# A vision-tower kernel on one core: the inverse root of both variances as one GpSimd power

## The reference

```python
h = _L0_tok_ref(x, L0_tok_channel_weights)          # sums of 16x16 patches, then 12 -> 192
h = h + _L0_attn_ref(_layernorm(h, axis=-1), L0_attn_W_qkv, L0_attn_b_qkv)
h = h + _L0_ffn_ref(_layernorm(h, axis=-1), ...)    # 192 -> 768, GELU, 768 -> 192
# _layernorm: (x - m) / sqrt(v + 1e-05)
```

## Time and profile before

| | |
|---|---|
| median of the runs | 500.92 us (500.5 to 501.59) |
| the profiled execution | 501.24 us |
| its span | 499.4 us |
| TensorE matmul busy | 426.2 us, 85% |
| VectorE busy | 415.4 us, 83% |
| ScalarE busy | 311.1 us, 62% |
| GpSimd busy | 338.3 us, 68% |
| moved by DMA | 166.74 MB, mean 334 GB/s |
| granted TensorE clock, mean | 0.952 |

### The profile page before, as it was taken

The page is one execution under the profiler, slowest core; times in us unless marked ns, Lnnn a source line. Parts: engine busy times, 40 slices in busy tenths (PEclk is TensorE's granted clock), DMA queues, the critical chain, the costliest instruction groups (busy, mean ns, idle before and its releaser), DMA issues.

```text
span 499.4 us, 10230 instructions
## 1 busy us (share of the span) xinstructions
PE 426.2 (85%) x3794; PEld 369.5 (74%) x3794; DVE 415.4 (83%) x392; ACT 311.1 (62%) x765; POOL 338.3 (68%) x637
## 2 busy tenths in 40 slices
PE   3994792878989898989898989898989898998897
PEld 2743451567878787879797878787878787887797
DVE  2767779999999999999999999999999999823100
ACT  1012021658686777777777777786868686868572
POOL 2021614286868686868787877878787868687981
PEclk9999556599999999999999999999999999999899
DMA  7999999999999999999999999999999993000011
GB/s 244 349 388 405 407 406 405 405 401 394 391 384 405 404 407 396 405 394 408 401 407 391 406 401 406 396 407 406 406 398 406 399 406 122 29 22 29 21 50 50
DMA packets 54028, 166.74 MB, mean 334 GB/s; under 512 B 6031, under 2 KB 6812, under 8 KB 53978
## 3 DMA queue, kind: packets, MB, share of 16 engines
q1 hardware_dynamic: 53978, 166.08, 85.8%
HBM read 156.42 MB, written 9.63 MB: 333 GB/s over the span
## 4 chain that ended last, share of the span: by engine, by line
DVE 68%; PE 18%; issue 6%; ACT 3%; POOL 3%; DMA 1%; SPq 1%; DVEq 0%; POOLq 0%
DVE pooled L414 52%; PE ps L577 16%; DVE phat_tok L453 5%; DVE stat L444 5%; DVE stat L435 1%; DMA xs<-x 1%; DVE prod L432 1%; DVE stat L446 1%; DVE stat L426 1%; ACT probs_t L960 1%; DVE prod L423 1%; DVE stat L447 1%; POOL stat L1110 0%; POOL newton L1106 0%; POOL newton L1108 0%
## 5 line engine op out<-in xcount | busy, mean ns | idle before, releaser
L414 DVE TENSOR_REDUCE pooled<-xs 128x28 f32<-128x1792 f32 x192 | 329.9, 1776 | 9.2 <-DMA xs<-x 9.2
L1158 POOL TENSOR_TENSOR h_lo<-h_f,h_hi 128x448 fp32r<-128x448 f32 (+1 forms) x192 | 193.1, 1033 | 68.9 <-ACT h_hi L1010 68.8
L577 PE MATMUL ps<-w_hi,h_hi 128*112 128x192 f32 x672 | 183.0, 272 | 0.4 <-POOL h_lo L1158 0.4
L577 PE MATMUL ps<-w_hi,h_lo 128*112 128x192 f32 x672 | 176.0, 262 | 0.0
L577 PE MATMUL ps<-w_lo,h_hi 128*112 128x192 f32 x672 | 176.0, 262 | 0.0
L577 PEld LDWEIGHTS ps<-w_hi,h_hi 128*112 128x112 f32 x672 | 119.8, 178 | 8.7 <-issue 7.2
L1009 ACT ACTIVATE h_f<-ps 128x448 f32<-128x448 f32 (+1 forms) x192 | 98.0, 511 | 37.8 <-PE ps L577 35.7
L577 PEld LDWEIGHTS ps<-w_lo,h_hi 128*112 128x112 f32 x672 | 119.7, 178 | 1.7
L577 PEld LDWEIGHTS ps<-w_hi,h_lo 128*112 128x112 f32 x672 | 120.2, 179 | 0.0
L1010 ACT ACTIVATE h_hi<-ps 128x448 fp32r<-128x448 f32 (+1 forms) x192 | 98.1, 511 | 0.0
L577 PE MATMUL ps<-uhat_stack,f_stack 128*128 128x448 f32 (+1 forms) x192 | 76.6, 400 | 1.4 <-ACT h_hi L1010 1.4
(11 more groups left out here) (144 smaller groups left out, 607.5 us busy)
## 6 DMA issues: line engine op xcount, KB each, us to landing
xs<-x SPq DMA_DIRECT2D x336, 448.0 KB, 7.6
out<-out_sb SPq DMA_DIRECT2D x16, 336.0 KB, 8.5
out<-out_sb SPq DMA_DIRECT2D x16, 252.0 KB, 6.7
out_sb<-wfc SPq DMA_DIRECT2D x1, 576.0 KB
wproj_sb<-wproj SPq DMA_DIRECT2D x1, 576.0 KB
wqkv_sb<-wqkv SPq DMA_DIRECT2D x1, 432.0 KB
cf<-const_full SPq DMA_DIRECT2D x1, 400.5 KB, 3.3
h_f<-const_paired SPq DMA_DIRECT2D x1, 153.0 KB, 3.7
```

The source lines that it names most:

```text
L414: dve.tensor_reduce(pooled[n % 2][:, t, GRID * low:GRID * high].rearrange("p (i j) -> p i j", j=GRID), rows, AX.XY, ALU.add).then_inc(redu ...
L577: return pe.matmul(o, a, b, start=start, stop=stop)
L1158: pool.tensor_tensor(h_lo[:, t, columns[part]], h_f32[:, unit % 4, 0:width[part]], h_hi[:, t, columns[part]].bitcast(F32), ALU.subtract).t ...
```

## The change

Epsilon becomes a further column of `prod`: 13 columns are summed for the first norm and 26 for the second, the last of them filled with epsilon once. `statistics` on VectorE (three small operations an iteration) is gone, and the twelve Newton operations of GpSimd are replaced by one `tensor_tensor` with `ALU.pow` of the variances and a tile of -0.5. GpSimd now waits for the sums themselves. Since that power reads `stat` row 0, `norm1` and `norm2` wait for the power of the iteration before (`root_steps`) before they write it again. `VAR` is 1.0, so the scaled masks keep their values; `SECOND`, `THIRD`, `THIRD_REST` and `MAGIC` are not used.

```diff
--- before.py
+++ after.py
@@ -83,7 +83,11 @@
 
 SLOTS = len(PIECES) * TILES
 LAG = 4
-MAGIC = float(0x5F3759DF)
+VAR = 1.0
+SECOND = 3.0 * VAR
+THIRD, THIRD_REST = 40.0 * VAR ** 3 / 3.0, 80.0 * VAR ** 6
+ROOT_OPS = 1
+MAGIC = float(0x5F3759DF + int(np.log2(VAR) * 2 ** 22) - 2 ** 31)
@@ -117,9 +121,8 @@
     },
 }
 DVE_ORDER = {
-    "statistics": 3,
     "loop": {
-        "reduce": (0, 4, 5, 6, 7, 8, 11, 12, 13, 14, 15, 17), "maxima": (81, 82), "context": 88, "norm1": 73,
+        "reduce": (0, 3, 4, 5, 6, 7, 10, 11, 12, 13, 14, 16), "maxima": (80, 81), "context": 87, "norm1": 73,
         "norm2": 146,
     },
 }
...
@@ -214,13 +217,12 @@
         u_four = sb("u_four", [HALF, 2, GROUP, 4, Q])
         uhat_tok = sb("uhat_tok", [HALF, 2, GROUP, BASIS])
         uhat_four = sb("uhat_four", [HALF, 2, GROUP, 4, Q])
-        prod = sb("prod", [HALF, 2, 2, GROUP, BASIS])
-        stat = sb("stat", [HALF, 4, 2, 2 * GROUP])
-        newton = sb("newton", [HALF, 2, 2 * GROUP])
+        prod = sb("prod", [HALF, 2, 2, GROUP, BASIS + 1])
+        stat = sb("stat", [HALF, 2, 2, 2 * GROUP])
+        minus_half = sb("minus_half", [HALF, 2, 2 * GROUP])
         phat_rows = sb("phat_rows", [128, TOKENS])
         b_rows = sb("b_rows", [128, TOKENS])
         probs_t = sb("probs_t", [HALF, GROUP, 2, TOKENS])
-        three_halves = sb("three_halves", [HALF, 2, 2 * GROUP])
         zero = sb("zero", [128, 1])
         row_inv = sb("row_inv", [HALF, 2, GROUP])
         warmed = sb("warmed", [128, 2 * GROUPS])
...
@@ -418,34 +419,29 @@
 
                 if first(m):
                     dve.wait_ge(setup_pool_self, 10)
+                    dve.memset(prod[:, 0, :, :, CHANNELS], VAR * EPS)
+                    dve.memset(prod[:, 1, :, :, BASIS], VAR * EPS)
                 dve.wait_ge(p_tok_ready, m + 1)
                 gram = ps[0:HALF, 0, 0:4 * COLS].rearrange("p (h g b r) -> p h g b r", h=2, g=2, b=GROUP)
                 dve.tensor_tensor(prod[:, 0, :, :, 0:CHANNELS], p_tok[:], gram[:, :, 1],
                                   ALU.mult).then_inc(norm1_multiplied, 1)
                 dve.wait_ge(norm1_multiplied, m + 1)
-                dve.tensor_reduce(stat[:, 0, 0, :], prod[:, 0, :, :, 0:CHANNELS].rearrange("p h b r -> p (h b) r"),
+                if not first(m):
+
+                    dve.wait_ge(root_steps, ROOT_OPS * m)
+                dve.tensor_reduce(stat[:, 0, 0, :], prod[:, 0, :, :, 0:CHANNELS + 1].rearrange("p h b r -> p (h b) r"),
                                   AX.X, ALU.add).then_inc(norm1_summed, 1)
 
             def norm2(m):
                 dve.wait_ge(g2_summed, m + 1)
                 gram2 = ps[0:HALF, 1, 0:256].rearrange("p (h b r) -> p h b r", h=2, b=GROUP)
-                dve.tensor_tensor(prod[:, 1], u_tok[:, :, :, 0:BASIS], gram2[:, :, :, 0:BASIS],
+                dve.tensor_tensor(prod[:, 1, :, :, 0:BASIS], u_tok[:, :, :, 0:BASIS], gram2[:, :, :, 0:BASIS],
                                   ALU.mult).then_inc(norm2_multiplied, 1)
                 dve.wait_ge(norm2_multiplied, m + 1)
+
+                dve.wait_ge(root_steps, ROOT_OPS * (m + 1))
                 dve.tensor_reduce(stat[:, 0, 1, :], prod[:, 1].rearrange("p h b r -> p (h b) r"),
                                   AX.X, ALU.add).then_inc(norm2_summed, 1)
-
-            def statistics(n, on):
-
-                if 1 in on:
-                    dve.wait_ge(norm1_summed, n)
-                if 2 in on:
-                    dve.wait_ge(norm2_summed, n - 1)
-                dve.tensor_scalar(stat[:, 1], stat[:, 0], EPS, None, ALU.add).then_inc(stat_steps, 1)
-                dve.wait_ge(stat_steps, 2 * n - 1)
-                dve.tensor_scalar(stat[:, 3], stat[:, 1], -0.5, None, ALU.mult)
-                dve.tensor_scalar(stat[:, 2].bitcast(I32), stat[:, 1].bitcast(I32), -0.5, MAGIC,
-                                  ALU.mult, ALU.add).then_inc(stat_steps, 1)
 
             def maxima(m, pair):
                 b = slice(2 * pair, 2 * pair + 2)
...
@@ -1077,7 +1071,7 @@
                 pool.memset(u_tok[:, :, :, ONE_U:ONE_U + 1], 1.0).then_inc(setup_pool_self, 1)
                 pool.memset(halves(uhat_four)[:, :, 0::2, ONE_F:ONE_F + 1], 1.0).then_inc(setup_pool_self, 1)
                 pool.memset(zero[:], 0.0).then_inc(setup_pool_self, 1)
-                pool.memset(three_halves[:], 1.5).then_inc(setup_pool_self, 1)
+                pool.memset(minus_half[:], -0.5).then_inc(setup_pool_self, 1)
                 pool.wait_ge(setup_pool_self, 10)
 
             def setup_wproj():
@@ -1093,22 +1087,18 @@
                 pool.wait_ge(setup_act, ACT_W1)
                 pool.tensor_tensor(w1_lo[:], w1_f32, w1_hi[:].bitcast(F32), ALU.subtract).then_inc(setup_pool, 1)
 
-            inv_std = stat[:, 2].rearrange("p k (h b) -> p k h b", h=2)
-
-            def inverse_roots(n):
-
-                at = 12 * (n - 1)
-                pool.wait_ge(stat_steps, 2 * n)
-                h, y = stat[:, 3], stat[:, 2]
-                for step in range(3):
-                    pool.tensor_tensor(newton[:], y, y, ALU.mult).then_inc(newton_steps, 1)
-                    pool.wait_ge(newton_steps, at + 4 * step + 1)
-                    pool.tensor_tensor(newton[:], newton[:], h, ALU.mult).then_inc(newton_steps, 1)
-                    pool.wait_ge(newton_steps, at + 4 * step + 2)
-                    pool.tensor_tensor(newton[:], newton[:], three_halves[:], ALU.add).then_inc(newton_steps, 1)
-                    pool.wait_ge(newton_steps, at + 4 * step + 3)
-                    pool.tensor_tensor(y, y, newton[:], ALU.mult).then_inc(newton_steps, 1)
-                    pool.wait_ge(newton_steps, at + 4 * step + 4)
+            inv_std = stat[:, 1].rearrange("p k (h b) -> p k h b", h=2)
+
+            def inverse_roots(n, on):
+
+                at = ROOT_OPS * (n - 1)
+                if 1 in on:
+                    pool.wait_ge(norm1_summed, n)
+                if 2 in on:
+                    pool.wait_ge(norm2_summed, n - 1)
+                var, y = stat[:, 0], stat[:, 1]
+                pool.tensor_tensor(y, var, minus_half[:], ALU.pow).then_inc(root_steps, 1)
+                pool.wait_ge(root_steps, n)
 
             def scale_p(m):
@@ -1186,7 +1176,7 @@
             def iteration(n, on):
                 for step in range(STEPS):
                     if step == POOL_ORDER["inverse_roots"] and (1 in on or 2 in on):
-                        inverse_roots(n)
+                        inverse_roots(n, on)
                     for k in sorted(on, reverse=True):
                         m, now = n - k, STEPS * k + step
                         at = order(POOL_ORDER, m)
```

More of the change, by code:

```diff
@@ L129 @@
 ACT_SETUP = {"coef": (0, 0), "basis": (0, 1), "w1": (1, 8), "w0t": (1, 8), "f": (1, 25)}
-DVE_SETUP = {"gram": (0, 0), "scores": (0, 8), "basis": (0, 8), "g2": (0, 14),
-             "biases": (0, 17), "resid": (1, 11), "f": (1, 18)}
+DVE_SETUP = {"gram": (0, 0), "scores": (0, 7), "basis": (0, 7), "g2": (0, 13),
+             "biases": (0, 16), "resid": (1, 10), "f": (1, 17)}
 POOL_SETUP = {"wproj": (0, 0), "w1": (1, 10), "w0t": (1, 10)}
@@ L143, in constants @@
     block = np.kron(np.eye(GROUP), np.ones((Q, Q)))
-    full[:, MASK_G:MASK_G + 128] = block / EMBED
+    full[:, MASK_G:MASK_G + 128] = block * (VAR / EMBED)
     full[:, MASK_S:MASK_S + 128] = block / np.sqrt(EMBED)
@@ L167, in constants @@
             paired[PLANES * t + plane[p], 128 * (2 * t + half[p]) + p] = 1.0
-    paired[:, PAIR_MASK:] = np.kron(np.eye(GROUP), np.ones((CHANNELS, CHANNELS))) / EMBED
+    paired[:, PAIR_MASK:] = np.kron(np.eye(GROUP), np.ones((CHANNELS, CHANNELS))) * (VAR / EMBED)
     return full, rows, paired
@@ L270, in build @@
         norm2_summed = sem("norm2_summed")
-        stat_steps = sem("stat_steps")
-        newton_steps = sem("newton_steps")
+        root_steps = sem("root_steps")
         phat_tok_ready = sem("phat_tok_ready")
@@ L563, in iteration @@
                             norm2(m)
-                    if step == DVE_ORDER["statistics"] and (1 in on or 2 in on):
-                        statistics(n, on)
                     for piece, build_piece in SETUP.items():
```

## The result

The changed kernel takes 480.61 us (median of four runs, 479.64 to 481.62) against 501.25 us of the kernel before; the ratio is 0.9588, 95% interval 0.9558 to 0.9619. The forecast was 478.0, with a range of 468 to 490. The profiled execution took 479.64 us, its span is 477.9 us: 21.5 less than before, where 23.15 were forecast. (The median lies 1 us above the profiled execution: two of the four runs took 479.7 and two 481.5.)

What follows compares the result with a forecast made beforehand. VectorE bounds the loop, with TensorE and DMA close behind; loads bind later. Span 499.4 - 19.35 (u_tok earlier) - 3.8 (program's end) = 476.25, plus 1.84 gives 478.1, rounded 478.0 us; range 468 to 490.

Steps and rivals of the forecast that it cites:

- VectorE sets the pace, and an operation of it stands still behind GpSimd: Loop: VectorE busy 25.36 of 25.60 us; the first small statistics operation takes 1.57 instead of 0.17, waiting for GpSimd's run.
- 1.87 of a period, new period 23.7 to 23.8: Loop on VectorE: the statistics' 1.87 us go from 25.55, leaving 23.7, plus 0.1 granted for waits.
- Loads set another end: Loop: at 406 GB/s loads finish only 3.9 us earlier, so DMA binds from about group 12.
- the two ends (478.0 and 469.7): Whole run: 478.0 us if loads bind late; 469.7 if VectorE binds to the end, a rival given 15%.
- the reserve of 11 us: Early loop: loads land some 11 us before they are wanted; 1.4 us used per period, gone some eight periods later.
- The last load lands at 411.7, u_tok 1.35 behind it at 413.05: End of loads: after the last landing at 411.7 us, u_tok is ready at 413.05, 19.35 earlier than before.
- The end of the program loses 3.8: TensorE's work after u_tok: a 0.36 us phat wait, 2.25 idle before uhat and 1.2 of slow clock go, together 3.8.
- x: Duration of the new GpSimd power: taken as 0.9 us, bounded by 0.22 and 3.6, hidden in the loop up to 3.7.
- idle stretch gone: Sign at the program's end: TensorE's idle 2.25 us before uhat is turned would disappear, as GpSimd starts 2.8 earlier.
- The clock term: Program's end: the slow stretch behind TensorE's idle time, granted clock 0.60, goes; counted as 1.2 us.
- slow power: Rival, 8%: above 3.7 us the GpSimd power delays the maxima, above 5.6 it loses 16 times the excess; 537 at 8.
- Landing times grow from 7 to above 15: Sign in the loop: time of loads from issue to landing rises from 7 us to above 15.

Runs made afterwards that it cites:

- b2: Kernel before, its three VectorE statistics operations written as one-element reductions and GpSimd's twelve Newton operations as multiplications of the same shape; 481.33 us, ratio 0.9607.
- c1: Kernel before with statistics moved from step 3 to step 4, one reduction later on VectorE; 491.07 us, ratio 0.9782.
- a1: Changed kernel with a chain of twelve GpSimd multiplications in place of the power, leaving out the inverse root; 481.56 us, ratio 0.9606.
- a2: Changed kernel with one GpSimd multiplication in place of the power, leaving out the inverse root; 478.7 us, ratio 0.9552.
- b3: Changed kernel with a second power of the same shape into a spare tile ahead of the real one; 538.63 us, ratio 1.0759.

## Why the prediction was right

- *VectorE sets the pace, and an operation of it stands still behind GpSimd.* Right, and shown from two sides: with another form (b2) and another place (c1) the stall goes and most of the time with it.
- *1.87 of a period, new period 23.7 to 23.8.* Measured 23.62 up to iteration 9.
- *Loads set another end.* Right: light loads take 9.3 us more off. The forecast put 8.35 between the two ends (478.0 and 469.7). They bind from group 10 and not 12. One of the two is the 0.1 to 0.2 by which the period came out below the 23.8 that was used there (11 us then last seven periods and not eight); the other is that the reserve of 11 us was a little too large.
- *The last load lands at 411.7, u_tok 1.35 behind it at 413.05.* They were at 412 to 413 and at 413.93. The rate was 407 and not 406, but at the very end it runs out over 5 us (295 GB/s from 407 to 408, 49 from 412 to 413), which the sum left out. And the path was another: the last reduction that waited for its load started at 401.04, and from its start to u_tok VectorE had 12.9 of its own work, with the five reductions before u_tok in one run (404.74, 8.78). The last landing held nothing up, since its slot was wanted only at 413.84. That the sum came within 0.9 of u_tok is partly luck.
- *The end of the program loses 3.8.* It lost 3.0. This is the term that x touches: x was taken as 0.9 and is 2.9, so 1.36 of TensorE's idle 2.25 stayed, as the prediction's own 3.7 - x gives it (2.25 - 0.8), and its sign "idle stretch gone" did not come. The clock term was put at 1.2 and is 1.6: from the turn of uhat to the end of the span 28.3 passed before (471.09 to 499.4) and 26.7 now (451.18 to 477.9). The 0.8 missing here and the 0.9 by which u_tok is late are the whole 1.65 between the forecast of the span (476.25) and the span.
- *x.* The value was wrong by a factor of three, the bounds (0.22 to 3.6) held it, and the sum hardly saw it since the loop hides it, as a1 and a2 show: from x = 0.22 to 3.6 the time goes up by 2.9, where the prediction had 2.3. That a value wrong by a factor of three cost so little is no merit of the estimate. The rival "slow power" had its threshold about right (3.7, and some 3.4 in b3) but too flat a slope: at x = 5.9 it gives 16 x 0.3, some 5 us more than before, and b3 took 37 us more (538.63 against 501.0). It had no term for the clock behind the wait. The first power of the changed kernel is no longer than the others (GpSimd in order of time):

```profile
47.36 2.92 POOL L1100 TENSOR_TENSOR stat<-stat,minus_half 98x16 f32<-98x16 f32 x1 [10.21 <-DVE stat L432]
```

The Trainium skill (GPSIMD Engine Reference, section 2.1, Instruction dispatch) gives some 6 us for the first call to a freshly loaded kernel. Nothing of that shows here.

- *Landing times grow from 7 to above 15.* Wrong. They go to 13 and stay:

```profile
L356 SPq DMA_DIRECT2D xs<-x x336: 534/934/2423, 3.2 to 398.0; - x168
...
DMA to landing us min/median/max: 4.9/13.0/15.0
```

and the row of the kernel before to it:

```profile
L355 SPq DMA_DIRECT2D xs<-x x336: 534/603/2240, 3.2 to 407.9; - x168
```

(Columns: minimum, median and maximum of the issue in ns, first and last start.) The issue itself takes 934 ns in the median instead of 603. So a slot also waits at SyncE before its load is on its way. VectorE's last reduction of slot 11, and SyncE's last loads (this view counts their issues as one run):

```profile
389.16 3.16 DVE L415 TENSOR_REDUCE pooled<-xs 128x14 f32<-128x896 f32 x2
```

```profile
383.70 15.23 SPq L356 DMA_DIRECT2D xs<-x  x15
```

The slot is free at 390.2 (its reduction takes 1.07, the other of the two is slot 0), and its load, the last of all, starts at 398.0: 7.8 at SyncE, and then some 13 to landing. A reader who takes the period less the landing time as the reserve, as the prediction did, sees too much of it.

## What to carry to other kernels

When a small operation has a mean far above its shortest, find what its neighbour engine does in just that time; changing its form or its place may be worth as much as removing it. When an engine that sets the pace gets faster, compute how long it can run ahead of the transfers, since that reserve decides how much of the gain arrives. A hidden chain costs nothing up to a threshold, and beyond it can cost more than its own time, through the clock.

## What the runs showed of the hardware

- A VectorE `tensor_scalar` from SBUF to SBUF, 98x16 float, takes 0.17 us alone, and while GpSimd is in its subtractions it ends only with them (1.57 to 3.38 us). A `tensor_reduce` of that shape is not held up (0.17 us, in the middle of the same pair). The Trainium skill (SBUF — State Buffer, section Who interferes with whom) says that `tensor_scalar` can take the port pair that VectorE shares with GpSimd, so that one of the two blocks, and that `tensor_reduce` on trn2 never contends. The runs agree on both (1.57 against 0.17 us). By that section the pair is held for one instruction; in the earlier trace rows the addition outlasts the second of two GpSimd subtractions, the first of which was running when it started.
- A GpSimd `pow` on floats takes 2.915 us for 98x16 and 1.65 us for 98x8, against 0.22 us for a multiplication of 98x16.
- Behind an idle 2.54 us of TensorE (b3, up to 225.50) the granted clock was at its lower level, 1.2 GHz, from 227.4 to 229.8 us at the least (0.50 in the row above). Behind an idle 1.36 us at the end of the changed kernel and an idle 2.03 us in a1 it was 1.00 over the 4 us shown.
- In the changed kernel the 16 DMA engines moved 407 GB/s over 310 us with outputs among the loads, and the time from issue to landing was 13.0 us in the median and 15.0 at most.
